# Moving the next value tile's taps between a chunk's masks and its gram products on VectorE, and the chunk's exponent ahead of the tanh on ScalarE

## The reference

```
q = l2_norm(silu(conv4(x @ Wq.T)))       # 16 heads of 64, causal convolution of 4 taps
k = l2_norm(silu(conv4(x @ Wk.T)))
v = silu(conv4(x @ Wv.T))                # 16 heads of 128
alpha = exp(-exp(A_log) * softplus(x @ Wa.T + dt_bias))
beta  = 2 * sigmoid(x @ Wb.T)
for each token t:                        # per sequence and head, S is 64 x 128
    S = alpha_t * (S - beta_t * k_t (k_t S)) + k_t v_t
    o_t = S q_t
x = x + rms_norm(o) @ Wo.T
```

## Time and profile before

| | |
|---|---|
| median of 3 runs | 7472.01 us (7466.28 to 7480.6) |
| the profiled execution: its time, its span | 7487.58 us, 7484.5 us |
| busy: PE / DVE / ACT / POOL | 6325.5 / 4573.0 / 2618.9 / 2267.8 us (85% / 61% / 35% / 30%) |
| mean granted clock of PE | 0.917 of full speed |
| DMA | 226.37 MB, mean 30 GB/s |

### The profile page before, as it was taken

The page is one execution under the profiler, slowest core; times in us unless marked ns, Lnnn a source line. Parts: engine busy times, 40 slices in busy tenths (PEclk is TensorE's granted clock), DMA queues, the critical chain, the costliest instruction groups (busy, mean ns, idle before and its releaser), DMA issues. The chain is left out here.

```text
span 7484.5 us, 162627 instructions
## 1 busy us (share of the span) xinstructions
PE 6325.5 (85%) x60192; PEld 4574.5 (61%) x60192; DVE 4573.0 (61%) x9685; ACT 2618.9 (35%) x5275; POOL 2267.8 (30%) x3893
## 2 busy tenths in 40 slices
PE   7888888988889888888888888788888888888887
PEld 4665746656566665656657566565755657566575
DVE  6556675665756657565566656657556575655664
ACT  3334242332424325243242423324233252432421
POOL 2513224151331514215133241423315133151321
PEclk9899998999989999898988989899899998999998
DMA  1110001011010110001100010110101010011100
GB/s 53 33 38 22 27 31 38 29 28 34 21 36 29 32 41 22 23 29 32 41 22 27 31 36 31 22 40 21 35 29 32 30 33 23 29 32 41 22 27 5
DMA packets 376536, 226.37 MB, mean 30 GB/s; under 512 B 336896, under 2 KB 353920, under 8 KB 367488
## 3 DMA queue, kind: packets, MB, share of 16 engines
q1 hardware_dynamic: 375680, 215.29, 9.9%
HBM read 156.54 MB, written 58.72 MB: 29 GB/s over the span
## 5 line engine op out<-in xcount | busy, mean ns | idle before, releaser
L1580 PE MATMUL PS<-BIG 64*64 64x128 f32 (+3 forms) x23200 | 1094.5, 260 | 235.9 <-PEq L2026 105.5
L827 DVE SCALAR_TENSOR_TENSOR PS<-BIG,CW,PS 128x512 f32<-128x512 f32 x1536 | 1155.8, 753 | 215.6 <-DVEq L825 137.3
L1580 PEld LDWEIGHTS PS<-BIG 64*64 64x64 f32 (+2 forms) x23200 | 933.1, 138 | 379.9 <-issue 368.6
L1580 PE MATMUL PS<-XT,BIG 128*128 128x512 f32 x2048 | 1068.4, 655 | 50.1 <-PEq L1891 50.1
L1583 PE MATMUL PS<-CST,BIG 128*128 128x128 f32 x3536 | 558.5, 296 | 312.8 <-PEq L1658 82.8
L1583 PEld LDWEIGHTS PS<-CST,BIG 128*128 128x128 f32 x3536 | 415.8, 149 | 434.6 <-issue 417.8
L1243 POOL TENSOR_TENSOR FR<-MS,NHALF 128x8 f32<-128x8 f32 x128 | 209.9, 1640 | 1485.2 <-POOLq L1242 1303.7
L1580 PEld LDWEIGHTS PS<-XT,BIG 128*128 128x128 f32 x2048 | 400.7, 207 | 399.5 <-issue 390.3
L1089 POOL TENSOR_TENSOR RSTD<-VAR,NHALF 128x2 f32<-128x2 f32 x202 | 142.3, 704 | 1602.0 <-POOLq L1088 1595.3
L1580 PE MATMUL PS<-BIG,CST 128*128 128x256 f32 (+1 forms) x1360 | 507.8, 519 | 112.1 <-PEq L1961 98.9
L1171 POOL TENSOR_TENSOR BIG<-BIG 128x30 f32<-128x30 f32 (+14 forms) x960 | 499.9, 521 | 136.4
(11 more groups left out here) (152 smaller groups left out, 10194.1 us busy)
## 6 DMA issues: line engine op xcount, KB each, us to landing
BIG<-in_wv SPq DMA_DIRECT2D x16, 2048.0 KB, 7.4
BIG<-in_wo SPq DMA_DIRECT2D x16, 2048.0 KB, 8.7
BIG<-in_wq SPq DMA_DIRECT2D x16, 1024.0 KB, 4.9
BIG<-in_wk SPq DMA_DIRECT2D x16, 1024.0 KB, 7.6
cells_in<-BIG SPq DMA_DIRECT2D x128, 128.0 KB, 2.7
BIG<-cells_in SPq DMA_DIRECT2D x32, 512.0 KB, 3.7
cells_out<-BIG SPq DMA_DIRECT2D x32, 512.0 KB, 2.6
cells_nat<-BIG SPq DMA_DIRECT2D x32, 512.0 KB, 3.6
```

The costliest lines, as they stand in the source:

```text
L827: op = v.scalar_tensor_tensor(y, pre[:, j:j + G], CW[:, i * TAPS + j:i * TAPS + j + 1], y, ALU.mult, ALU.add)
L1580: return nc.tensor.matmul(out_, l, r, start=start, stop=stop)
```

## The change

Nothing is added or left out: the engines issue the same instructions in another order. On PE, `grams` and `decays` move one tile later, and `grams(c - 2)` now stands ahead of the projection of tile i. On DVE, `grams(c - 1)` stands behind the taps of tile i. On ACT, `exponents` is split: the exponent of bank 5 stands ahead of the tanh and the one of bank 7, now `gammas`, behind it, both one tile later. POOL's and SP's lists stay as they are.

```diff
@@ DVE, projections
-                    if 0 <= c - 1 < CHUNKS:
-                        grams(c - 1)
                     y, pre = conv_bank(i), PRE[i % 4]
...
                             op.then_inc(conv_ready, 1)
+                    if 0 <= c - 1 < CHUNKS:
+                        grams(c - 1)
                     if i > 0:
                         conv_finish(i - 1)
@@ ACT, exponents
                 a.activation(bank(5), bank(5), ACT.Exp).then_inc(dm_ready, 1)
+
+            def gammas(c):
                 act.wait_ge(gam_bank, 1)
@@ ACT, projections
+                    if 0 <= i - PREP - 1 < CHUNKS:
+                        exponents(i - PREP - 1)
                     if 0 < i <= CONV_TILES:
                         tanh_of(i - 1)
+                    if 0 <= i - PREP - 1 < CHUNKS:
+                        gammas(i - PREP - 1)
...
-                    if 0 <= i - PREP < CHUNKS:
-                        exponents(i - PREP)
@@ PE, projections
+                    if 0 <= c - 2 < CHUNKS:
+                        grams(c - 2)
                     for k in range(KT):
...
-                    if 0 <= c - 1 < CHUNKS:
-                        grams(c - 1)
...
-                    if 0 <= c < CHUNKS:
-                        decays(c)
+                    if 0 <= c - 1 < CHUNKS:
+                        decays(c - 1)
```

## The result

The changed kernel takes 7526.12 us (median of 4 runs, 7515.11 to 7546.85) against 7473.61 (4 runs, 7466.28 to 7480.6) for the kernel before: a ratio of 1.0074, 95% interval 1.005 to 1.0098. It is slower by some 55 us by the ratio (52.5 by the medians), where 7473 was predicted and 7493 was the upper end of the range. The profiled execution took 7546.85 us with a span of 7544.3, which is 59.8 more than the span before.

What follows compares the result with a forecast made beforehand. POOL's chain to the inverse, following DVE's grams of chunks 3, 4, 5 and 7, was taken to bound each group; terms over the 16 groups, -2.7 + 1.4 + 0.5 + 1.6 = +0.8 us, gave 7473, range 7454 to 7493.

Steps and rivals of the forecast that it cites:

- the part on the wait that takes the place: DVE's chunk loop: next masks wait for PE's decays, 0.06 stall; statistics add 1.3 in chunks 1 and 2, normalisation 0.93.
- the old gap: DVE's idle time ahead of the gram products (L897), 140.9 us in all, which the change aimed to remove.
- Its own sign of being wrong: POOL's copy over 1 us off 84.04 behind the group's first masks, or a wait at L2089 that has not grown.
- the chain: POOL's substitution to copy, SP's spill, PE's inverse: sets a group's time, following DVE's grams of chunks 3, 4, 5, 7.
- the end of the chunk stage: PE reaches L2089 about 5 us earlier and waits about 8.5 instead of 3.5; worth nothing.
- the chain up to chunk 4: DVE's masks and gram products, chunks 0 to 4: products of chunk 4 at 2010.97 instead of 2010.34, taken as 0.5 later.
- Its +0.8 us for the whole: POOL's gains and losses summed over the 16 groups: -2.7 + 1.4 + 0.5 + 1.6.
- the first masks: DVE's masks of chunk 0, behind a projection and ACT's copies: 1975.47 against 1975.07, 0.4 later.
- The clock at 0: PE's granted clock behind L2089: the longer wait for the inverse was costed at 0.
- The full gain: Rival: inverse not last, so 5 us a group show, 16 x 5 = 80, 7392; chance 0.05.
- the clock: Rival: longer wait keeps PE at the lower level behind L2089, ten more groups, 40 us, 7513; chance 0.08.
- later grams: Rival: products 1.04 further behind the masks; lower clock on chunks 0 to 4 adds 1.2 a group, 7493; chance 0.14.

Runs made afterwards that it cites:

- experiment 10: Changed kernel with each of POOL's two sums cut into two instructions of 128x256: 7507.1 us, ratio 1.0044 to the kernel before.
- experiments 3 and 4: POOL's forward substitution for chunks 0 to 3 left out, in the changed kernel (3): 7298.56 us, and in the kernel before (4): 7349.18 us.
- experiment 1: Changed kernel with the statistics of chunks 1 and 2 and normalisation of chunks 4 and 5 moved behind the taps: 7488.33 us, ratio 1.0014.
- experiments 2 and 6: Extra PE matmuls ahead of the wait for the inverse: 2, six a group in the changed kernel, 7497.14 us; 6, three in the kernel before, 7445.47 us.

## Why the prediction was wrong

**The failed step** is in the part on the wait that takes the place: "The statistics of chunks 1 and 2 filled the old gap [...], and now stand in the chain with 1.3" and "The normalisation of chunk 4 costs 0.93". Both durations came from rows in which POOL's sums lay elsewhere. In their new place they measured 0.85 more in chunk 1 (16 groups), the same in half the groups in chunk 2, and 1.34 more in chunk 4: 2.6 a group, 42 us of DVE time, on the path that sets the end. The prediction moved DVE's instructions but left POOL's where they were, though what releases POOL's sums, ACT's exponent of bank 7 behind PE's decays, is among the things that it did move. Its own sign of being wrong came: POOL's copy starts 85.21 behind the first masks in the fifth group instead of 84.04, and the first substitution comes 2.65 later on average, not 0 to 1.

The trace of the kernel before held a hint, in chunk 5 of the fifth group, DVE and POOL:

```profile
2017.17 0.89 DVE L504 TENSOR_SCALAR BIG<-XB,MVR,RSTD 128x256 f32<-128x256 f32 x2 [0.21 <-DVEq L502]
```

```profile
2017.83 1.14 POOL L1184 TENSOR_TENSOR BIG<-ST,CST 128x512 f32<-128x512 f32 x1 [0.24 <-POOLq L1203]
```

Here the second of the two normalisations starts first, 0.17 ahead of the sum. It keeps its 0.40, and the sum lasts 1.14 instead of 1.04. So it is in 12 groups (1.13 or 1.14); in the other four the two do not meet, and the sum lasts 1.04 or 1.05.

The Trainium skill has the rule that fits ("SBUF — State Buffer", "Who interferes with whom"): VectorE and GpSimd share a pair of ports as an exclusive lock, a `tensor_scalar` can take it, and whoever comes second stands still for the other's whole instruction. The traces agree, down to the end of the add at the end of the sum (2008.59 and 2008.57), to the sum of 1.14 in the opposite order and to the halves of experiment 10. The prediction did not weigh it.

**Right:** the chain. POOL's substitution, copy and SP's spill end last in all 16 groups; the end of the chunk stage was given back at PE's wait (118.7 us, 110 to 150 predicted), and experiments 3 and 4 show the 50 us that lie behind it. That the wait fell into its range is in part luck: PE came to it 2.2 a group earlier, not 5 (91.59 behind the first masks, 93.82 before), and the inverse 1.7 later (99.01 and 97.33), where it was to stay within 0.1. With the collisions gone, in experiment 1, PE comes 5.2 earlier and waits 7.74. L886 has 76.4 us (60 to 110). POOL got back 0.63 a group between substitution and copy; predicted were 0.2 and up to 0.6.

**Right in size, as experiment 1 shows:** the chain up to chunk 4. By the prediction's numbers its products start 2010.97 - 1975.47 = 35.50 after the first masks; with the collisions gone they start at 35.46. The agreement is closer than its parts: the single terms are off by -0.29 to +0.10 and cancel. The cycles it gave were 7.63, 8.10, 8.10 and 6.95; the changed kernel has 7.34, 9.00, 8.64 and 7.05, the excess in the two with the add. Its +0.8 us for the whole would then be +10 (1.0014), inside its own range of -10 to +15. These 10 us are not assigned to any step; the first masks, which the prediction had 0.4 later, come 0.84 later in experiment 1 (behind the first finish of a value tile), which would make 7 of them, but no run tests it.

**The clock at 0** holds for the difference. With a wait of 7.74 in experiment 1 the stretch behind the inverse takes 13.46, with 3.50 before 13.70: the longer wait costs no more there than the short one. The 1.06 more in the changed kernel's profile (six groups that stay low for over 15 us, before five) account for some 4 of the 55 us by experiments 2 and 6 (55 - 51; the intervals of these two runs allow some 13 either way). What the prediction missed is that the loss was there to be recovered in the kernel before: 10.22 instead of 13.70 for three matmul calls that nobody reads. Here the rule that it weighed, that an idle engine starts its next burst at half clock (the Trainium skill, "TensorE: Matmul & The Clock Gate", "HAM oscillation — how this bites in real kernels"), agrees with the runs.

**The rivals.** The full gain (7392) and the clock (7513) fell as causes, later grams (7493) too. The lower level that this last one needed did come in 11 of the 16 groups, some 15 us behind the first masks (mean granted clock 0.96 from 4 us ahead of these to the products of chunk 4, 1.00 in the other five). In the fifth group the decays of chunk 2 take it, 4.39 instead of 2.82:

```profile
2011.65 4.39 PE L1584 MATMUL PS<-BIG,CST 128*128 128x512 f32 x8 [2.15 <-PEq L1965]
```

But chunk 4 comes at 37.99 on average in these groups and at 38.11 in the other five, so it is not the loss. In experiment 1 the clock is at the higher level there in all 16 groups. The time lies beyond all of them, because the mechanism was on no list.

## What to carry to other kernels

When an instruction moves, look at what then runs beside it on the other engines, and move on paper also whatever is released by it: a duration read from a trace holds only beside the same neighbours. An instruction that got longer shows in no list of waits; compare the mean of each line and form, and the same instruction's duration from place to place. And a wait that cannot be removed on TensorE can still be filled: keeping it busy there was worth 31 to 35 us in the kernel before.

## What the runs showed of the hardware

- A VectorE `TENSOR_SCALAR` on 2 elements a partition, 0.17 us alone, took 0.93 to 1.02 beside a GpSimd `TENSOR_TENSOR` of 128x512 and ended 0.02 to 0.03 behind it (24 of 24); one of 128x256 took 1.02 to 1.13 instead of 0.41, and 0.60 to 0.70 beside 128x256. Where the `TENSOR_SCALAR` had started first, it kept its 0.40 and GpSimd's instruction took 1.13 or 1.14 instead of 1.04. Taps, masks and products, which have an operand in PSUM (0.68 to 0.76), and the batch-norm instructions (0.41 to 0.43, 0.15 to 0.18) kept their durations.
- TensorE's granted clock behind a wait was the lower level whether it had stood for 3.5 or 7.4 us, and came back 6 to 18 us after work began again; with extra matmuls up to 1.3 to 3.1 us ahead of the inverse (experiment 2) the lower level was short (10.9 to 12.3 from the inverse to the recurrence in 11 of 16 groups) or did not come at all (five groups, four of them at 9.27).
